# Plain fp32 matmuls for the second attention's scores, and another order between the attentions

## The reference

```python
x = layernorm(x + attn(x))            # 32 heads of 16, 8 key heads, causal, rotary
x = layernorm(x + xattn(x, ctx))      # 32 heads of 128, 8 key heads, rotary by position_ids, mask
x = layernorm(x + ffn(x))             # x @ weight.T + bias, kept where softmax cluster hits allow
# xattn, per batch b and head h:
scores = q[b, h] @ k[b, h // 4].T / sqrt(128); scores = where(mask == 0, -1e9, scores)
x = softmax(scores) @ v[b, h // 4]; return concat_heads(x) @ Wo
```

## Time and profile before

| | us |
|---|---|
| median of 3 runs (lowest, highest) | 792.45 (791.98, 793.5) |
| the profiled execution | 796.18 |
| its span, first to last instruction | 794.4 |
| mean granted clock of TensorE | 0.984 |

### The profile page before, as it was taken

The page is one execution under the profiler, slowest core; times in us unless marked ns, Lnnn a source line. Parts: engine busy times, 40 slices in busy tenths (PEclk is TensorE's granted clock), DMA queues, the critical chain, the costliest instruction groups (busy, mean ns, idle before and its releaser), DMA issues.

```text
span 794.4 us, 13805 instructions
## 1 busy us (share of the span) xinstructions
PE 764.3 (96%) x4809; PEld 652.7 (82%) x4809; DVE 596.3 (75%) x1143; ACT 323.4 (41%) x684; POOL 404.6 (51%) x381
## 2 busy tenths in 40 slices
PE   6799999989999999999999999999999999999996
PEld 4688888888878888888888888888888888887874
DVE  4689999887877777686677768667776866686777
ACT  4566666633432423342333334233333423333335
POOL 7667767754654444464444445454444535354303
PEclk9799999999999999999999999999999999998998
DMA  7710004022343222222332222233222222240002
GB/s 183 195 33 18 17 17 122 5 63 68 87 120 95 79 54 81 54 53 53 98 76 64 79 53 53 53 91 72 75 79 53 54 53 81 48 110 3 2 0 107
DMA packets 107876, 53.56 MB, mean 67 GB/s; under 512 B 80448, under 2 KB 96960, under 8 KB 107840
## 3 DMA queue, kind: packets, MB, share of 16 engines
q1 hardware_dynamic: 107008, 51.51, 25.5%
q10 hardware_dynamic: 576, 1.05, 0.4%
q0 software_dynamic: 256, 0.52, 0.3%
HBM read 32.62 MB, written 2.10 MB: 44 GB/s over the span
## 4 chain that ended last, share of the span: by engine, by line
PE 66%; DVE 16%; POOL 6%; issue 6%; ACT 2%; DMA 2%; SPq 1%; DVEq 0%; POOLq 0%; ACTq 0%
PE bank L767 18%; PE bank L702 15%; PE bank L506 10%; DVE arena_r L1693 5%; PE s_bank L781 4%; PE bank L530 2%; PE s_bank L783 2%; PE bank L751 2%; DVE small L1789 2%; PE bank L587 2%; PE bank L927 2%; PE s_bank L751 1%; DVE arena_f L1777 1%; POOL arena_f L1553 1%; DMA arena_f<-in_L_attn_Wo 1%
## 5 line engine op out<-in xcount | busy, mean ns | idle before, releaser
L767 PE MATMUL bank<-arena_r 128*128 128x512 f32 x768 | 193.9, 402 | 0.0
L1036 ACT ACTIVATE arena_r<-bank 128x256 fp32r<-128x256 f32 (+2 forms) x249 | 105.3, 460 | 205.7 <-PE bank L734 84.4
L702 PE MATMUL bank<-arena_r 128*128 128x512 f32 x720 | 185.3, 400 | 1.6 <-POOL arena_r L1534 1.1
L767 PEld LDWEIGHTS bank<-arena_r 128*128 128x128 f32 x768 | 141.3, 191 | 27.5
L702 PEld LDWEIGHTS bank<-arena_r 128*128 128x128 f32 x720 | 130.6, 188 | 31.0 <-POOL arena_r L1534 1.5
L506 PE MATMUL bank<-arena_r 128*128 128x256 f32 (+1 forms) x1056 | 147.0, 294 | 2.3 <-DVE arena_r L1693 1.5
L506 PEld LDWEIGHTS bank<-arena_r 128*128 128x128 f32 x1056 | 137.2, 191 | 10.2 <-DVE arena_r L1693 3.4
L1693 DVE TENSOR_TENSOR arena_r<-bank,arena_r 128x256 fp32r<-128x256 f32 (+2 forms) x217 | 99.5, 484 | 42.9 <-ACT arena_r L1036 42.1
L1036 ACT ACTIVATE arena_r<-arena_f 128x512 fp32r<-128x512 f32 (+1 forms) x178 | 104.0, 638 | 60.6 <-DMA arena_f<-arena_f 44.5
L1693 DVE TENSOR_TENSOR arena_r<-arena_f,arena_r 128x512 fp32r<-128x512 f32 (+1 forms) x95 | 89.4, 949 | 15.4 <-ACT arena_r L1036 15.0
L1525 POOL TENSOR_TENSOR arena_f<-arena_f 128x512 f32<-128x512 f32 x30 | 39.2, 1308 | 113.9 <-DVE arena_f L1882 113.8
(11 more groups left out here) (164 smaller groups left out, 1191.3 us busy)
## 6 DMA issues: line engine op xcount, KB each, us to landing
arena_f<-arena_f SPq DMA_DIRECT2D x120, 128.0 KB, 2.5
arena_f<-in_L_xattn_Wo SPq DMA_DIRECT2D x8, 1024.0 KB, 5.7
arena_f<-in_L_xattn_Wq SPq DMA_DIRECT2D x14, 512.0 KB, 4.0
arena_f<-in_x SPq DMA_DIRECT2D x8, 256.0 KB, 3.0
arena_f<-in_x SPq DMA_DIRECT2D x1, 2048.0 KB, 10.1
arena_f<-in_L_xattn_Wk SPq DMA_DIRECT2D x8, 256.0 KB, 3.0
arena_f<-in_L_xattn_Wv SPq DMA_DIRECT2D x8, 256.0 KB, 3.3
arena_f<-in_ctx SPq DMA_DIRECT2D x8, 256.0 KB, 3.1
```

The source lines that it names most:

```text
L702: mm = pe.matmul(BQ2[f][:], w2q_s[a][:, e, j, f, :], xT[b][:, e, tok], start=(e == 0 and n == 0), stop=(e == EC - 1 and n == 2))
L767: mm = pe.matmul(BO2[i][:], at2[a][:, h, i * P:(i + 1) * P], w2o_s[b][:, h, :], start=(h == 0 and n == 0), stop=(h == HG - 1 and n == 2))
L1036: act.activation(dst, src, ACT.Copy).then_inc(done, 1)
```

## The change

Scores become one plain fp32 matmul per head pair and batch, of the staged queries by keys in fp32. The copies and low parts of queries and keys and the corrections go, ACT copies the scores out whole. SyncE waits for the scores before it overwrites the staging buffer of j = 1. `cT` is laid out by tile. Between the attentions TensorE takes the first query product ahead of the transposes of tile 7, and context turns and half of the keys and values ahead of the first attention's values; ACT, DVE and GpSimd follow in their orders. The diff, cut:

```diff
-        kT2 = cut(r2.take(4 * P), i=2, n=2 * P)
-        sc2, corr2 = f2.take(512), f2.take(512)
+        sc2, kT2 = f2.take(512), f2.take(512)[:, 0:2 * P]
@@ sync, slot
                 if is_unit(u + 3):
+                    if j == 1:
+                        sp.wait_ge(c_s, u + 2)
                     stage_q(u + 3, j, cp)
@@ tensor
-            return banks[0] if isinstance(v, int) and v >= T - 2 else banks[7]
+            return banks[0] if isinstance(v, int) and v == T - 1 else banks[7]
-            def scores(u, first):
-                pe.wait_ge(c_ql, 2 * u + 2)
-                pe.wait_ge(c_kl, u + 1)
+            def scores(u, c, first):
+                pe.wait_ge(d_qs, staged(u, c))
+                pe.wait_ge(c_kh, u + 1)
                 if not first:
                     pe.wait_ge(c_al, 3 * u)
-                for h in range(2):
+                for j in range(2):
                     for b in range(4):
-                        at = 2 * b * S
-                        high, low_ = (w[:, h, b].rearrange("p h q -> p (h q)") for w in qT2)
-                        pe.matmul(BS2[h][:, at:at + 2 * S], high, kT2[:, :, b * S:(b + 1) * S],
-                                  start=True, stop=False, skip_group_check=True)
-                        mm = pe.matmul(BS2[h][:, at + S:at + 2 * S], low_, kT2[:, 0, b * S:(b + 1) * S],
-                                       start=False, stop=True, skip_group_check=True)
+                        mm = pe.matmul(BS2[j][:, b * S:(b + 1) * S],
+                                       staged_q(u, c, j)[:, b].rearrange("p h q -> p (h q)"),
+                                       kT2[:, b * S:(b + 1) * S], start=True, stop=True)
@@ tensor, between the attentions
             v = T - 1
+            pe.wait_ge(s_x1l, 2)
+            pe.wait_ge(c_wql, 4)
+            q_proj(0, 0, 0)
+            q_proj(0, 0, 1).then_inc(c_q, 1)
             pt_stage(v, 0)
             pt_stage(v, 1)
-            pe.wait_ge(s_res, v)
-            for j in range(2):
-                q_proj(0, j, 0)
-                q_proj(0, j, 1).then_inc(c_q, 1)
-            pt_stage(v, 2)
-            pt_stage(v, 3)
-            pv_stage(v, 0, False)
-            pv_stage(v, 1, False)
             pe.wait_ge(s_cp, 4 * T)
             ctx_turn(0)
             ctx_turn(1)
-            pe.wait_ge(c_rq, 1)
-            wo_stage(v, v, False)
+            q_proj(0, 1, 0)
+            q_proj(0, 1, 1).then_inc(c_q, 1)
+            pt_stage(v, 2)
+            pt_stage(v, 3)
...
+            kv_proj(0, 0)
+            pv_stage(v, 0, False)
+            pv_stage(v, 1, False)
             pe.wait_ge(c_xl, 2)
-            kv_proj(0, 0)
             kv_proj(0, 1).then_inc(c_kv, 1)
+            pe.wait_ge(c_rq, 1)
+            wo_stage(v, v, False)
             x1_stage(v - 1, None, banks[7])
@@ scalar
-                copy(cut(corr2, x=8, k=S), s_pairs[:, :, 1, :], c_cr)
+                if not starts_with(u):
+                    act.wait_ge(c_sub, u)
+                copy(cut(sc2, h=2, n=4 * S), cut(s_banks, h=2, n=512)[:, :, 0:4 * S], c_cr)
@@ scalar, slot
-                corrections(u)
+                scores_copy(u)
...
-                    q_high(u + 1, c1, 0)
-                    q_high(u + 1, c1, 1)
@@ gpsimd, tile_steps of the last tile, then its slot, then between the attentions
                 sub(i, 0, not old)
+                    wq_low(0, 2)
                 sub(i, 1, not old)
+                    wq_low(0, 3)
...
-                    wq_low(0, 0)
-                    wq_low(0, 1)
...
-                if is_unit(u + 3):
-                    sum_q(u + 3)
                 if starts_with(u):
                     wq_low(1, 0)
                     wq_low(1, 1)
+                if is_unit(u + 3):
+                    sum_q(u + 3)
...
             norm(v, 2)
+            wkv_low(0, 0)
+            wkv_low(0, 1)
             norm(v, 3)
@@ vector
-                dve.tensor_tensor(cut(sc2, x=8, k=S), s_pairs[:, :, 0, :], cut(corr2, x=8, k=S), ALU.add).then_inc(c_ad, 1)
...
-                    q2_low(u + 1, c1, 0)
-                    q2_low(u + 1, c1, 1)
-                    k2_low(u + 1)
@@ vector, between the attentions
+            rope_first(0, 0)
             p_low(v, 0)
             total(v, 3)
             p_low(v, 1)
+            ctx_low(0)
+            ctx_low(1)
             p_low(v, 2)
             p_low(v, 3)
             rope_first(0, 1)
             stats1(v - 1)
             moments1(v - 1)
+            norm1(v - 1)
             at_low(v)
-            ctx_low(0)
-            ctx_low(1)
-            norm1(v - 1)
+            rope2_k(0, 0, True)
             add1(v)
```

More of the change, by code:

```diff
@@ L123, in decoder_layer @@
         w2o_s = [cut(v, h=HG, n=E) for v in parts(r2, HG * E)]
+        cT = [cut(v, t=T, c=EC, n=P) for v in parts(r2, EC * B * S)]
         qT2 = [cut(v, j=2, b=4, h=2, q=S) for v in parts(r2, HG * 2 * P)]
-        cT = [cut(v, c=EC, n=B * S) for v in parts(r2, EC * B * S)]
-        kT2 = cut(r2.take(4 * P), i=2, n=2 * P)
+        r2.take(4 * P)
         v2 = [[cut(v, i=2, n=D2) for v in parts(r2, 2 * D2)] for _ in range(2)]
@@ L226, in decoder_layer @@
         c_q, c_kv, c_rq, c_rk, c_qs, c_ks = (sem(n) for n in ("c_q", "c_kv", "c_rq", "c_rk", "c_qs", "c_ks"))
[L227 to L230, removed]
+        c_vh, c_vl, c_kt, c_kh = (sem(n) for n in ("c_vh", "c_vl", "c_kt", "c_kh"))
+        c_mask = sem("c_mask")
+        c_s, c_cr, c_cp, c_mx, c_sub, c_ex = (
+            sem(n) for n in ("c_s", "c_cr", "c_cp", "c_mx", "c_sub", "c_ex"))
         c_sum, c_rc, c_pn, c_pt, c_ph, c_pl = (sem(n) for n in ("c_sum", "c_rc", "c_pn", "c_pt", "c_ph", "c_pl"))
@@ L554, in pv_stage @@
                     pe.wait_ge(s_vl, v + 1)
-                    if is_last(v):
-                        pe.wait_ge(s_al, v)
-                    elif not first:
+                    if not first:
                         pe.wait_ge(s_res, v)
@@ L827, in slot @@
                 if kv_next:
-                    scores(u + 1, False)
+                    scores(u + 1, c1, False)
             pe.wait_ge(s_init, 1)
@@ L878, in _ @@
             q_pair(1, 1, 1)
-            scores(0, True)
+            scores(0, 0, True)
             pe.wait_ge(s_x1l, v)
@@ L948, in _ @@
             fw_turn(1)
-            scores(v + 1, False)
+            scores(v + 1, (v + 1) % UN, False)
             v = U - 2
@@ L1196, in ctx_high @@
                 act.wait_ge(c_xT, t + 1)
[L1197 to L1206, removed]
+                copy(cT[0][:, t, :, :], ctx_bank(t)[:].rearrange("p (c n) -> p c n", c=EC), c_xh)
             def k_high(u):
                 act.wait_ge(c_kt, u + 1)
-                copy(kT2[:, 0, :], banks[3][:, 0:2 * P], c_kh)
+                copy(kT2, banks[3][:, 0:2 * P], c_kh)
             def v_high(u, c):
@@ L1247, in slot @@
                     ctx_high(2 * c1 + 1)
-                    exponents(u)
-                if kv_next:
-                    q_high(u + 1, c1, 0)
-                    q_high(u + 1, c1, 1)
-                if not turns_ctx(u + 1):
-                    exponents(u)
+                exponents(u)
                 if c == 0:
@@ L1295, in _ @@
             v = T - 1
-            for u in range(4):
-                p_high(v, u, False)
-            at_high(v, False)
+            p_high(v, 0, False)
+            p_high(v, 1, False)
             ctx_high(0)
             ctx_high(1)
+            p_high(v, 2, False)
+            p_high(v, 3, False)
+            at_high(v, False)
             act.wait_ge(s_x1n, v)
@@ L1358, in _ @@
             v = U - 2
-            corrections(v)
+            scores_copy(v)
             fw_high(2)
@@ L1507, in tile_steps @@
                 value_low(i)
-                if not ahead:
-                    wq_low(0, 0)
-                    wq_low(0, 1)
                 if old:
@@ L1603, in _ @@
             root1(v - 1)
-            wkv_low(0, 0)
-            wkv_low(0, 1)
             sum_k(0)
@@ L1805, in tile_steps @@
                 if not following:
+                    wq_low(0, 0)
+                    wq_low(0, 1)
                     masked_max(i, 0, False)
@@ L1808, in tile_steps @@
                     masked_max(i, 1, False)
-                    wq_low(0, 2)
                     at_low(v)
@@ L1814, in tile_steps @@
                     x1_low(w)
-                    wq_low(0, 3)
                     add1(v)
@@ L2008, in slot @@
                 if starts_with(u):
-                    k2_low(1)
                     values_low(1, 1)
@@ L2144, in _ @@
             at2_low_second(v)
-            k2_low(v + 1)
             values_low(v + 1, c + 1)
```

73 lines of the change are left out of this document (19 added, 54 removed).

## The result

| | before | after |
|---|---|---|
| median of the runs, us (first comparison, 9 runs each) | 792.45 | 786.11 |
| the two later comparisons, medians, us | 794.81 (23 runs) and 794.10 (13) | 786.23 (6) and 786.56 (8) |
| profiled execution: own time, span, mean granted clock | 796.18, 794.4, 0.984 | 784.15, 782.3, 0.996 |

The ratio of the first comparison is 0.9915, 95% interval 0.9892 to 0.9939; of the later ones 0.9896 (0.9864 to 0.9928) and 0.9912 (0.9879 to 0.9946). Predicted were 787.4 us, 783.8 to 790.9.

A forecast was written before the change was run, and what follows sets the result against it. TensorE was taken as the bound, busy 764.3 of 794.4 us. Terms -0.8 - 0.3 - 0.6 - 0.6 - 1.6 - 1.1 sum to -5.0 us, from 792.45 to 787.4 us; range 783.8 to 790.9.

The forecast's parts named there:

- The prediction's 0.2%: Difference, 1.6 us, taken as about what a measurement of this kernel tells from no change.
- Part 1, scores at 0: TensorE's score matmuls: 16 pairs at 0.11 us, 1.7 us per unit either way, so 0; bounds -3.6 to +9.7 us.
- fourth rival: Score matmuls: fp32 load and matmul pairs dearer, from 0.010 us more per pair; at 0.13 us 797.2 us; chance 0.05.
- The prediction's own sign of being wrong: Wrong if the loop's unit is longer than 17.4 us, or a half clock stands between 165 and 190 us.
- c = 0 units, 6 x 0.14: Six units where the values' products wait for DVE's p2_low: 0.14 us less each with DVE relieved, -0.8 us.
- 300.12: TensorE's wait at 300.12 us, the same as in c = 0 units, 0.22 idle plus 0.07, goes: -0.3 us.
- 648.30, 705.55, 720.21: TensorE's waits: at 648.30 ACT's staging-DMA wait goes, -0.6 us; at 705.55 and 720.21 scores stop waiting for k2_low, 0.33 each.
- SyncE's wait at 0: SyncE waits for the scores ahead of every second stage_q: taken as 0; +12 us if the cover were gone.
- Part 3, -1.6: Between the attentions: 3.0 us of TensorE idle less new waits of 0.75, 0.1 and 0.5 leaves 1.6 gained.
- Part 4, -1.1: First unit: GpSimd's two wq_low go ahead of sum_q(3), ending TensorE's 1.07 us idle at 221.46: -1.1 us.
- The rival of the half clock: The half clock from 721.3 to 728.1 us goes too, 3.4 us more gained, 784.0 us; chance 0.15.
- DVE near 505 us busy, ACT near 285: Expected signs: total busy times of DVE and ACT after the low parts, adds and query copies go.

The follow-up runs named there:

- order-only kernel: The new engine orders between the attentions and in GpSimd's first unit, put on the kernel before, scores still split fp32r: 789.3 us, ratio 0.9945.
- the two kernels with 1.9 us of wait: Output product moved ahead of the last scores but one, on split scores with the new orders, and on after with other waits filled too: the latter 786.16 us.

## Why the prediction was right, by its steps

The forecast's mechanism was right and its sum slightly small: -5.0 expected, -5.5 by the stages. The median of 786.11 lies 1.3 below 787.4, most likely since part of before's executions also hold the half clock near the end, which no profiled one of after showed. That it came so near is partly luck: the later comparisons differ by 8.6 and 7.5 us where this one has 6.3. The prediction's 0.2%, as what a measurement tells from no change, was set low as well: the intervals reach 0.23 to 0.34% to either side.

- *Part 1, scores at 0*: nearly. Start to next block is 1.70 us both times, 0.112 us per pair when doubled. What was missed is small: the product behind fp32 scores takes 2.851 us for 2.831, and the ordinary unit 17.45 for 17.43. 0.02 a unit, +0.6 us over the kernel. It is an eighth of the fourth rival's smallest price (0.010 x 16 = 0.16 us a unit), and it stands behind the pairs, not in their pitch; why is open. The prediction's own sign of being wrong, a unit over 17.4 us, was set too tight to be used: the ordinary unit of before took 17.43.
- *c = 0 units, 6 x 0.14*: 17.54 to 17.58 us became 17.45, 0.09 to 0.13 each, and 0.09 to 0.11 comes back in five of them when work is put back. Right; the stage of 16 units shows only 0.22, because the twelve others pay 0.02.
- *300.12*: the size was right (0.25 us in the order-only kernel). The reason, DVE's work, was incomplete: ACT's wait of 3.22 us for a staging transfer stands in the chain, and the work alone doesn't bring TensorE's wait back. The prediction read ACT's wait only at 648.
- *648.30, 705.55, 720.21*: between the order-only kernel and after these starts move up by 0.70, 0.27 and 0.29 us, counted from the start of the block ahead, where 0.6, 0.33 and 0.33 stood.
- *SyncE's wait at 0*: right; every unit of the loop takes 17.45 us.
- *Part 3, -1.6*: -1.91. The new waits came where they were put: 0.59 us for 0.75 at the fourth transposes, 0.30 for 0.1 at at_low, 0.51 for 0.5 at the add. The rest is the old 3.0 of idle, which was a little more. The first scores start at 187.25 + 3.38 (the start's difference) = 190.6, where 190.9 was forecast.
- *Part 4, -1.1*: -1.34 by putting it back.
- *The rival of the half clock* (0.15) came true in the first profiled executions (784.0 forecast, 784.15 measured), but its reason isn't shown. The fall is missing with the same 1.33 us of wait in one execution of before and present in one other and in the order-only one: two of three plain executions with split scores. It is missing in all eight with fp32 scores and waits of 1.06 to 1.30 us there. It is present at 2.68 us, and missing in the two kernels with 1.9 us of wait in front of the values' product some 12 us later. What is shown: the fall is not certain at a wait of 1.3 us, and a longer wait at that place brings it back. Whether the 0.3 us less made it rarer, or eight executions were lucky, is open. The sentence of the Trainium skill ("TensorE: Matmul & The Clock Gate", Part 4) that transposes don't count as busy doesn't decide it: the same transposes stood before both kinds of execution.
- *DVE near 505 us busy, ACT near 285*: wrong for DVE, 535; near for ACT, 289.5. Half of DVE's 30 us is in the last section. Most of the rest was in the forecast itself: 60 query low parts went and not 64, in all 52.3 us (78.2 - 25.9) where 58.9 were counted, and the keys' took 10.7 where 13.4 were. It cost TensorE nothing that the stages show.

## What to carry to other kernels

Cost an edit by the waits of the bound engine, one by one, with what comes late next: 61 us less of busy DVE were worth under 1 us (the c = 0 units), and single waits the rest. Where a kernel's runs vary by a few us, cut the trace into stages at the starts of the same blocks: these repeat to 0.1 us and settle what the medians can't. A gap ahead of the instruction that begins a latency chain (scores before a softmax) can't be filled with work that delays it, unless the end of the chain has slack.

## What the hardware showed that was not expected

The masked copy of a unit (COPY_PREDICATED, 128x512, same operands) took longer in after: group by shape of before, then of after, and one of each in DVE's and GpSimd's timelines.

```profile
L1942 DVE COPY_PREDICATED arena_f<-mask_i,small 128x512 f32<-128x512 int32 x32 | 26.2, 819 | 5.0 <-DVE arena_f L1939 5.0
...
413.62 0.85 DVE L1942 COPY_PREDICATED arena_f<-mask_i,small 128x512 f32<-128x512 int32 x1 [0.16 <-DVE arena_f L1939]
...
411.32 2.55 POOL L1534 TENSOR_TENSOR arena_r<-arena_f,arena_r 128x512 fp32r<-128x512 f32 x2
```

```profile
L1898 DVE COPY_PREDICATED arena_f<-mask_i,small 128x512 f32<-128x512 int32 x32 | 41.6, 1301 | 52.2 <-ACT arena_f L1028 52.2
...
405.80 1.53 DVE L1898 COPY_PREDICATED arena_f<-mask_i,small 128x512 f32<-128x512 int32 x1 [1.79 <-ACT arena_f L1028]
...
404.19 2.53 POOL L1510 TENSOR_TENSOR arena_r<-arena_f,arena_r 128x512 fp32r<-128x512 f32 x2
```

Without the add it starts earlier against GpSimd's subtractions: in before it began 0.25 us ahead of their end (411.32 + 2.55 = 413.87) and took 0.85 us, in after it began 0.92 ahead (406.72) and took 1.53. It ended 0.60 and 0.61 us after them. Where GpSimd is idle it takes 0.75 to 0.76 us (at 190.89 and 714.25 us of after). So the masked copy ends 2.29 us behind the start of ACT's copy of the scores where it ended 2.32 behind: in this unit the add's 0.84 us (412.78 to 413.62) are nearly all taken back. The whole traces show the same: in before and in after, 22 of the 32 masked copies began beside a GpSimd instruction, and each ended 0.60 to 0.63 us behind the end of that one. And 15.4 of the 30 us missing from DVE's forecast relief are this row. The Trainium skill ("SBUF — State Buffer", SBUF: two separate sides) says that VectorE and GpSimd arbitrate for a shared port pair by "an exclusive lock, not a bandwidth split". The 44 ends 0.6 us behind GpSimd's, whatever the start, agree with it.
